# Loading x behind the shift weights, and high parts first in the first K/V tile

## The reference

```
mod = silu(c) @ wmod                       # six vectors per batch: sa, ca, ga, sb, cb, gb
h   = layernorm(x) * (1 + ca) + sa
Xn  = layernorm(h) * gamma + beta
K, V, Q = Xn @ W_in + b_in                 # K and V then rotated
A   = 0.5 * sum_rows(K/|K| * V/|V|) + 0.5
x   = x + ga * ((A * Q) @ W_out + b_out + h)
h   = layernorm(x) * (1 + cb) + sb
x   = x + gb * (relu(h @ W_up.T) @ W_down.T + (sum of the top-2 softmax weights) * h @ W_expert)
```

## Time and profile before

| | us |
|---|---|
| median of 3 runs | 363.46 (363.29 to 365.01) |
| the profiled execution | 365.14 |
| its span | 363.4 |
| PE busy | 353.1 (97%) |
| DVE busy | 247.9 (68%) |
| ACT busy | 159.1 (44%) |
| POOL busy | 126.6 (35%) |
| DMA, 27.45 MB | mean 76 GB/s over the span |

### The profile page before, as it was taken

One profiled execution on the slowest core, in us unless ns is written; L12 is line 12 of the kernel. 1 busy time (PEld: TensorE's weight loads), 2 busy tenths in 40 slices (PEclk: granted clock), 3 DMA queues, 4 the chain that ended last, 5 costly groups with the idle time before them and its releaser, 6 DMA issues.

```text
span 363.4 us, 4952 instructions
## 1 busy us (share of the span) xinstructions
PE 353.1 (97%) x1794; PEld 288.5 (79%) x1794; DVE 247.9 (68%) x508; ACT 159.1 (44%) x301; POOL 126.6 (35%) x131
## 2 busy tenths in 40 slices
PE   8799999999999999999999999999999999999996
PEld 5257587788777788888888898988988898889885
DVE  2689999979977778786977469338623852382474
ACT  1296838647169501476018753444234423441110
POOL 0395879777726166243531324800100010000000
PEclk9999999999999999999999999999999999999999
DMA  6998482370120000000000003101100110011003
GB/s 182 388 406 317 194 318 89 137 213 0 25 63 2 0 2 29 1 1 2 0 31 0 0 2 115 32 0 58 60 0 2 58 59 2 0 60 58 2 1 115
DMA packets 10985, 27.45 MB, mean 76 GB/s; under 512 B 1216, under 2 KB 1600, under 8 KB 9808
## 3 DMA queue, kind: packets, MB, share of 16 engines
q1 hardware_dynamic: 10960, 27.13, 21.1%
HBM read 22.90 MB, written 4.23 MB: 75 GB/s over the span
## 4 chain that ended last, share of the span: by engine, by line
PE 60%; DVE 12%; ACT 8%; issue 7%; DMA 5%; POOL 5%; SPq 2%; POOLq 0%; DVEq 0%; ACTq 0%
PE ps L1225 19%; PE ps L1227 19%; PE ps L1226 19%; PE ps L1284 2%; DMA gate_bc<-mod_rows 2%; DMA xs<-in_X 2%; POOL w_lo L414 2%; DVE hb L815 1%; DVE hst L825 1%; ACT z L626 1%; POOL hrs L411 1%; ACT ps L638 1%; DMA mod_rows<-xs 1%; ACT ps L585 1%; ACT z L617 1%
## 5 line engine op out<-in xcount | busy, mean ns | idle before, releaser
L1225 PE MATMUL ps<-wv_hi,t_hi 128*128 128x260 f32 (+1 forms) x192 | 61.7, 322 | 0.9 <-POOL wv_lo L414 0.5
L1227 PE MATMUL ps<-wv_hi,t_lo 128*128 128x260 f32 (+1 forms) x192 | 61.4, 320 | 0.0
L1226 PE MATMUL ps<-wv_lo,t_hi 128*128 128x260 f32 (+1 forms) x192 | 61.4, 320 | 0.0
L1225 PE MATMUL ps<-w_hi,g_hi 128*128 128x512 f32 (+1 forms) x132 | 51.2, 388 | 0.0
L1225 PE MATMUL ps<-t_hi,w_hi 128*128 128x512 f32 x128 | 50.6, 396 | 0.1
L1227 PE MATMUL ps<-w_hi,g_lo 128*128 128x512 f32 (+1 forms) x132 | 50.6, 383 | 0.0
L1226 PE MATMUL ps<-w_lo,g_hi 128*128 128x512 f32 (+1 forms) x132 | 50.6, 383 | 0.0
L1227 PE MATMUL ps<-t_hi,w_lo 128*128 128x512 f32 x128 | 50.0, 390 | 0.0
L1226 PE MATMUL ps<-t_lo,w_hi 128*128 128x512 f32 x128 | 49.9, 390 | 0.0
L1225 PEld LDWEIGHTS ps<-wv_hi,t_hi 128*128 128x128 f32 x192 | 36.1, 188 | 5.1 <-POOL wv_lo L414 1.4
L411 POOL TENSOR_TENSOR hrs<-hve,expo 128x4 f32<-128x4 f32 (+2 forms) x12 | 11.1, 923 | 81.9 <-DVE hve L832 62.8
(11 more groups left out here) (153 smaller groups left out, 703.8 us busy)
## 6 DMA issues: line engine op xcount, KB each, us to landing
stage<-in_w SPq DMA_DIRECT2D x5, 1024.0 KB, 4.8
out<-xs SPq DMA_DIRECT2D x15, 256.0 KB, 2.0
xs<-in_X SPq DMA_DIRECT2D x3, 1024.0 KB, 9.5
xs<-in_wmod SPq DMA_DIRECT2D x8, 256.0 KB, 5.9
stage<-in_w SPq DMA_DIRECT2D x8, 256.0 KB, 8.1
xs<-in_wmod SPq DMA_DIRECT2D x2, 1024.0 KB, 7.7
gate_bc<-mod_rows SPq DMA_DIRECT2D x8, 256.0 KB, 3.9
gate_bc<-in_wmod SPq DMA_DIRECT2D x1, 1024.0 KB, 13.3
```

The source lines that it names most:

```text
L1225: mm(dst, l_hi, r_hi, start=start, stop=False)
L1226: mm(dst, l_hi, r_lo, start=False, stop=False)
L1227: return mm(dst, l_lo, r_hi, start=False, stop=stop)
```

## The change

The load of row tile 0 of x of batch 0 is issued behind the four chunks of the shift weights instead of in front of them. The last low part of the V weights (chunk 3) is taken from POOL's order, where it stood in front of `shift_h0(2)`, and put into DVE's, behind `h_row0(3)` and in front of `t0_split(1)`. K/V tile 0 gets its own order on PE, `first_tile`: for each chunk the two products with the high part of the K weights and of the V weights, which wait for the high parts only, with the transposes of row tile 1 at the second chunk as before; then, for each chunk, the product with the low part of K and of V, which wait for the low parts. The number of products is the same, 24. The split on DVE gets a second wait like its first.

```diff
--- before.py
+++ after.py
@@ -293,9 +293,9 @@
                 sp.dma_start(x_slot(0).rearrange("p (t d) -> p t d", t=NT)[:, rows0, :],
                              x_batch[0][:, rows0, :]).then_inc(x0_in[i], 16)
 
-            load_x0(0)
             for k in range(NC):
                 sp.dma_start(x_slot(3)[:, k * D:(k + 1) * D], wmod[0][:, k * D:(k + 1) * D]).then_inc(sa_w[k], 16)
+            load_x0(0)
             load_x0(1)
             sp.dma_start(idn[:], ident).then_inc(ident_in, 16)
             load_x0(2)
@@ -533,7 +533,6 @@
             low_kv(1, 1)
             low_kv(1, 2)
             low_kv(0, 3)
-            low_kv(1, 3)
             shift_h0(2)
             rstd_x(1)
             shift_h0(3)
@@ -1076,6 +1075,7 @@
             def split_lo_kv(i, k):
                 dve.wait_ge(whi_v if i else whi_k, k + 1)
                 dve.wait_ge(wlo_v if i else wlo_k, k)
+                dve.wait_ge(wlo_v if i else wlo_k, k)
                 v.tensor_tensor(w_lo_of(W_ORDER[i], k), w_raw[i][:, k * D:(k + 1) * D],
                                 w_hi_of(W_ORDER[i], k).bitcast(f32), ALU.subtract).then_inc(wlo_v if i else wlo_k, 1)
 
@@ -1111,6 +1111,7 @@
             split_lo_kv(0, 2)
             scale_row0(3)
             h_row0(3)
+            split_lo_kv(1, 3)
             t0_split(1)
             x_stats(1)
             x_aggr(1)
@@ -1284,6 +1285,22 @@
                     last = nc.tensor.transpose(ps[:, t_bank(g, c), t * P:(t + 1) * P], z[:, t, c * P:(c + 1) * P], idn[:])
                 last.then_inc(t_ps, 1)
 
+            def first_tile():
+                k_bank, v_bank = kv_pair(0, 0)
+                pe.wait_ge(t_los, 1)
+                for k in range(NC):
+                    if k == 1:
+                        transposes0(1)
+                    for bank, r, ready in ((k_bank, WK, whi_k), (v_bank, WV, whi_v)):
+                        pe.wait_ge(ready, k + 1)
+                        mm(ps[:, bank, :], t_hi[:, 0, k, 0:P], w_hi_of(r, k), start=(k == 0), stop=False)
+                        mm(ps[:, bank, :], t_lo[:, 0, k, 0:P], w_hi_of(r, k), start=False, stop=False)
+                for k in range(NC):
+                    for bank, r, split in ((k_bank, WK, wlo_k), (v_bank, WV, wlo_v)):
+                        pe.wait_ge(split, k + 1)
+                        last = mm(ps[:, bank, :], t_hi[:, 0, k, 0:P], w_lo_of(r, k), start=False, stop=(k == NC - 1))
+                last.then_inc(kv_ps, 1)
+
             def kv_tile(b, t):
                 prior = before_on_pair(b, t)
                 if prior is not None:
@@ -1295,8 +1312,8 @@
                     pe.wait_ge(mod_sb, 1)
                 banks = kv_pair(b, t)
                 for k in range(NC):
-                    if b == 0 and t < 2 and k == 1:
-                        transposes0(t + 1)
+                    if b == 0 and t == 1 and k == 1:
+                        transposes0(2)
                     if b == 0 and t == 2 and k == 2:
                         transposes0(3)
                     if b == 0 and k == 0:
@@ -1304,11 +1321,9 @@
                     if b > 0 and t == 0:
                         pe.wait_ge(t_los, b * NC + max(k + 1, 2))
                     lo, hi = t_lo[:, b % 2, k, t * P:(t + 1) * P], t_hi[:, b % 2, k, t * P:(t + 1) * P]
-                    for bank, r, split in zip(banks, (WK, WV), (wlo_k, wlo_v)):
+                    for bank, r in zip(banks, (WK, WV)):
                         if b > 0 and t == 0 and k == 0 and r == WV:
                             pe.wait_ge(a_sb, b)
-                        if t == 0:
-                            pe.wait_ge(split, k + 1)
                         last = three(ps[:, bank, :], hi, lo, w_hi_of(r, k), w_lo_of(r, k), k == 0, k == NC - 1)
                 last.then_inc(kv_ps, 1)
 
@@ -1342,8 +1357,10 @@
                     done.then_inc(o_ps, 1)
 
             def attention(b):
-                kv_tile(b, 0)
-                if b > 0:
+                if b == 0:
+                    first_tile()
+                else:
+                    kv_tile(b, 0)
                     out_rows_of(b - 1)
                 for t in range(1, NT):
                     if b == 0 and t == 1:
```

## The result

The changed kernel takes 365.34 us (median of 20 runs, 364.36 to 366.58), the kernel before, run beside it, 363.97 us (20 runs, 363.29 to 365.21). The ratio is 1.0037, with a 95% interval of 1.0027 to 1.0047: about 1.4 us slower. A later session gave 1.0046 (1.0030 to 1.0063). The forecast was 363.6 us, within 362.8 to 365.2, with an effect of +0.14 us.

The account below looks back on a forecast made before the run. PE, 97% busy, was taken to bound the kernel; +0.95 us on DVE, hidden by PE's new order and two port waits, left +0.14. Added to the 363.46 median: 363.6 us, range 362.8 to 365.2.

Parts of the forecast that it names:

- what becomes of DVE's delay: DVE from t_lo of tile 1 to the two rows at 48.15: delay absorbed, leaving +0.14 us in the span.
- two waits at the shared port: DVE's scaling at 36.12 and two rows at 48.15 wait for POOL, leaving DVE +0.47, then +0.14 us late.
- Part 1: x load: tile 0 lands at 12.44, 3.9 us later, making DVE's shifted row of tile 0 0.95 us later (+0.3 to +1.6).
- M: Start of DVE's statistics of x tile 1, from which early times are counted; 13.17 in the kernel before.
- Part 2: K/V tile 0 on PE, high parts first: most of 1.78 us of waiting goes, except 0.1 to 0.2.
- rival D: PE's stop before tile 0's transposes grows to 2.9 us and its clock falls: 1.7 us more, 365.3; chance 0.08.
- Part 3: Last V split on DVE waits for POOL at the port, taking 1.4 us, not 0.68; tile 2's transposes +0.14 us.
- A: DVE's delay is not taken up by the port waits and carries through: +1.0 us, 364.5; chance 0.18.
- B: x tile 0 lands by 11.4, so the load move costs nothing and tile 1 starts 0.9 earlier: 363.2; chance 0.12.
- C: K/V tile 0's stalls go whole and are handed on: 1.78 us less, 361.7; chance 0.04.
- another meeting at the port: Other meetings at the port with one POOL operation: +1.3 us, 364.9; chance 0.05.
- E: The change doesn't do what it says, only for the V split, as late as POOL's own; included in the forecast.

Follow-up runs that it names:

- c2: Only the load of x tile 0 moved behind the shift weights, against the kernel before: 366.04 us (7 runs), ratio 1.0041.
- c4: The whole change plus five filler products on PE in the stop ahead of tile 0's transposes: 365.70 us (6 runs), 1.0045 against the kernel before.
- d2: The whole change with port order fixed near 57 us and gate rows waited for one by one: 364.15 us, 0.9998 against the kernel before.
- e1: The whole change with a semaphore for each gate row, port order left to chance: 365.26 us, 1.0025 against the kernel before.
- e2: The whole change with DVE always first at the port near 58 us, gates waited for together: 364.87 us, 1.0018 against the kernel before.
- e3: The whole change, unaltered, run again in a later session: 365.85 us, 1.0046 against the kernel before.
- c1: The kernel before, unchanged, profiled a second time: 365.32 us (1 run).
- c3: New order of K/V tile 0 and V split on DVE, x load left as in the kernel before: 364.46 us, 1.0005 against that kernel.
- c6: Only the new order of K/V tile 0, x load and last V part as in the kernel before: 363.72 us, 0.9986 against that kernel.
- c8: The kernel before, with POOL's second low part of the output weights waiting until DVE has summed: 364.53 us, 0.9998 against the kernel before.
- c9: The kernel before, with a semaphore for each gate row so that each user waits for its own: 363.82 us, 0.9986 against the kernel before.
- d1: The kernel before with both port order fixed near 57 us and gate rows waited for one by one: 363.78 us, 0.9987 against the kernel before.
- d3: Only K/V tile 0's new order, with port order fixed and gate rows waited for singly: 363.56 us, 0.9976 against the kernel before.
- d4: The kernel before plus three long-fulfilled waits and a tiny fill on DVE where the change puts the V split; no run time given.
- c7: The whole change, but x tile 0 issued behind two of the four shift chunks: 364.07 us, 0.9991 against the kernel before.

## Why the prediction was wrong

The step that failed is the one on what becomes of DVE's delay: the forecast let the new order on PE and two waits at the shared port take up all but 0.14 us of it, and some 0.8 us reached DVE's sum near 57 us. The other parts first.

**Part 1, +0.95: right.** x tile 0 was let land at 12.44; its statistics started between 11.76 and 13.49 in the seven traces with the whole load moved (after, c2, c4, d2, e1, e2, e3), 12.41 on the mean. The predicted M is 13.17 + 0.95 = 14.12. The mean M of those seven is 14.08 (13.43 to 15.16), the mean of nine traces with DVE waiting for tile 1 (before, c1, c3, c6, c8, c9, d1, d3, d4) is 13.10: +0.98. c7 shows the same from the other side. What the prediction lacked was a look at the spread: the start that the landing of x tile 0 sets moves by 1.7 us between executions, and with the wait gone it goes whole into M, which reached 15.16.

**Part 2, the order on PE: right, with one event less likely than it was.** From M, the forecast had tile 2's transposes at 30.84 - 14.12 = 16.72. Where the clock held (c4) it is 16.80. In after it is 17.21, because rival D's event happened: the stop was 2.79 us (2.9 in the forecast), and the clock fell. I gave that 0.08; the granted clock fell in the profiles of after, d2, e1, e2 and e3, and 15 of the 20 runs of after show a mean of 0.995 or less, as does 1 of the 111 runs of before in the later sessions. It held in c2's profile, with a stop of 2.78 us, while 5 of c2's 7 runs show 0.995 or less, so such a stop doesn't decide it alone. Its price was put at 1.7 by halving. Measured at tile 2's transposes it was 0.41 in after (17.21 against 16.80), where the fall came behind tile 0's transposes and tile 1 had to wait for t_lo anyway, 0.45 in e1 and 1.65 in e2, where it came ahead of them and lasted longest; 0.10, 0.44 and 1.21 of these are left at 57 us. So D is real, and as dear on PE as I said in e2. But c4, and the five runs of after with a full clock, show that most of the loss is there without it. That D's 365.3 meets the measured 365.34 is luck.

**Part 3, the split at 1.4: right.** It took 1.54 at 26.75, beside POOL's 26.45 to 27.74. DVE was free for t_lo of tile 1 at M + 14.51 (28.21), predicted 28.64 - 14.12 = 14.52. The Trainium skill ("SBUF — State Buffer", section "Who interferes with whom") says that a DVE instruction with two SBUF inputs is kept out by a GpSimd instruction that reads SBUF and was first; here the trace agrees, with 1.54 against the 0.68 of the same split in after at 24.64.

**What becomes of DVE's delay: here the forecast failed**, in three steps.

First, the way from t_lo of tile 1 to t_lo of tile 2. I had the latter at +1.0 for a shift of 0.95, that is M + 20.36. It came at M + 20.75 (34.45). The 0.35 of the unforeseen stop and little else lies between. It moves DVE's string, POOL's rows behind it (36.25, M + 22.55, instead of M + 22.2) and, where PE is early, PE: in c4 two of its products start 0.39 apart instead of 0.23, at 35.32, where this t_lo is needed, and tile 3's transposes stood 7.66 behind tile 2's instead of 7.38. d4 shows that the added instructions alone bring this stop.

Second, "the two rows at 48.15, bound to POOL's four low parts, which start with ACT at +0.14, end at +0.14". They ended at +0.37 (52.00 against 51.63), as they arrived, and M was +0.53 in that trace: counted from M they are 0.16 earlier than in before, where the forecast has 0.81. Both halves of the sentence failed. POOL's parts began at M + 31.33, not at 44.94 - 14.12 = 30.82, and their end doesn't fix the rows' end: c7's ended 1.15 us ahead of it. Whether such a meeting takes up a delay depends on when the two engines arrive: the 0.37 of after went through whole, of the 1.03 more in c4 nothing did. The prediction named POOL's last part as the sign of this step, "if the Q parts end over 0.5 from 51.2"; it ended at 51.44 in after and 50.79 in c4, so the sign kept still while the step failed. The first meeting did take up something, as foreseen: +0.97 at t_lo became +0.53 behind it, in the first of the two port waits.

Third, "From there DVE and PE go on together, and all that follows is moved by the same amount". The shift at 57 us, counted as the forecast does it from equal landings, is +0.98 for M and 44.33 - 44.49 = -0.16 for the order, **+0.8 us instead of +0.14**. Behind 57 us there are two places that don't hand a shift on as it is: the meeting at 58 us, 0.04 us apart, that costs DVE 1.1 us when lost, and the wait for all gate rows near 78 us. The whole change lost 1.4 us as it is, and 0.4 with both places changed (d2 against d1). In the traces without the port edit DVE lost the meeting in 1 of 7 (before, c1, c3, c6, c7, c9, d4) with an early x and in 2 of 5 (after, c2, c4, e1, e3) with a late one; that is too few to say that the change turns it. So the 0.6 us between +0.8 and +1.4 hang on these two places, but how it is shared between them, and in what execution each strikes, stays open. Of d2's +0.64 at 57 us against d1, 0.47 are left at 172 us and 0.18 from 261 us on, so in this pair a part of the shift is also swallowed later, at places that I did not follow up.

**The rivals.** A, the delay goes through DVE whole, 364.5: nearest to what happened, both in mechanism and in size, and given 0.18. Against it I had set that "two of those instructions only wait"; the first of them did take up 0.4. B's condition (tile 0 landed by 11.4) was true in no trace of the change; c7 made it true, and lost nothing. C was held up by t_lo of tile 1, as said there: c4's PE waits 0.19 for it. The case of another meeting at the port, +1.3 with 0.05, has its counterpart in the one at 58 us, which costs 1.1 and was lost in 3 of 12 traces. E gives the forecast's own number and isn't told apart from it.

**The base.** 363.46 was the median of three runs, and the same kernel has 363.97 over 20. Half a microsecond of the distance between 363.6 and 365.34 is that. The rest, 1.23 us, is what the effect was missed by: 1.37 instead of 0.14.

## What to carry to other kernels

A load may be moved back by as much as its first user waits anyway, no more, and this slack must be taken at its smallest over executions, not from one trace: here 2.45 us of slack met a delay of 3.9, and a move of half as far cost nothing. An engine that "waits anyway" at a shared port takes up a delay for sure only if what it waits for is fixed in time; where it stands behind whatever the other engine is doing as it arrives, 0.4 us went through whole here and 1.0 us was taken up, by how the two happened to meet. Compare traces by distances from the last landing that sets the order, and medians over many runs for the whole, since two spans of single executions can have the wrong sign.

## What was not expected of the hardware

The granted clock fell to 0.50 in or behind a stop of PE of 2.74 to 3.01 us in five profiles (after, d2, e1, e2, e3), and not with stops of 1.2 us, or of 1.6 in c7, nor with the 2.78 of the profiled c2. In after it fell 1.3 us behind the end of the stop and came back at 23.2, in e2 it fell 0.8 us ahead of the end and came back at 25.5, so that nearly the same stop cost 0.4 or 1.65 us at tile 2's transposes.

Two instructions on DVE and POOL that start 0.04 to 0.05 us apart in each of the 12 traces without the port edit, and of which one is held up by the other, go ahead now the one, now the other, with no sign in their recorded starts: 1.02 against 2.15 us for the same DVE instruction (c1 against before).

A fill of 0.07 us, with three waits that were long fulfilled, brought a stop of 0.35 us in DVE's stream 4.9 us and several instructions later, in d4, as the split did in after.

The landing of x tile 0, issued last of the same five loads, moved by 1.7 us between executions: DVE started on it between 11.76 and 13.49 us, in seven traces.
